# Attention decay on two engines: a split by diagonal block and rest in place of a split by key tile, and no mask matmuls in the transposed score pass

## The reference

```
scores = einsum('bhqd,bhkd->bhqk', q, k) / sqrt(8)
logw   = -log1p(softplus(decay_raw)[h] * log1p(max(q - k, 0)))
att    = softmax(scores + causal + logw[h])      # causal: -inf where k > q
y      = einsum('bhqk,bhkd->bhqd', att, v) @ w_proj
```

## Time and profile before

| | us |
|---|---|
| median of 3 runs | 771.75 (770.9 to 772.74) |
| span of the profiled execution, first to last instruction | 769.8 |
| TensorE busy | 648.5 (84%) |
| VectorE busy | 494.0 (64%) |
| GpSimd busy | 435.7 (57%) |
| ScalarE busy | 312.7 (41%) |

### The profile page before, as it was taken

The page is one execution under the profiler, slowest core; times in us unless marked ns, Lnnn a source line. Parts: engine busy times, 40 slices in busy tenths (PEclk is TensorE's granted clock), DMA queues, the critical chain, the costliest instruction groups (busy, mean ns, idle before and its releaser), DMA issues.

```text
span 769.8 us, 14013 instructions
## 1 busy us (share of the span) xinstructions
PE 648.5 (84%) x4380; PEld 427.1 (55%) x4381; DVE 494.0 (64%) x1115; ACT 312.7 (41%) x399; POOL 435.7 (57%) x295
## 2 busy tenths in 40 slices
PE   0392716999999899999899999998799999999950
PEld 0191415565665556666566656664376766767630
DVE  8618504887778677877678777786344544545535
ACT  3560003556555455555456555556222222222210
POOL 5210773686777667777577877787133333434332
PEclk9999856999999999999999999999699999999985
DMA  9920210021111111110111111013511111111119
GB/s 202 168 100 14 66 52 21 19 51 29 36 39 39 28 42 33 28 50 26 32 45 28 49 27 37 26 26 124 144 39 49 52 48 50 47 46 54 53 61 280
DMA packets 48299, 45.40 MB, mean 59 GB/s; under 512 B 6878, under 2 KB 38368, under 8 KB 47984
## 3 DMA queue, kind: packets, MB, share of 16 engines
q1 hardware_dynamic: 43888, 36.14, 19.4%
q0 software_dynamic: 4352, 8.47, 3.4%
HBM read 17.13 MB, written 17.44 MB: 45 GB/s over the span
## 4 chain that ended last, share of the span: by engine, by line
PE 80%; DVE 10%; another core or an unknown queue 3%; issue 2%; DMA 2%; POOL 1%; SPq 0%; ACT 0%; DVEq 0%; POOLq 0%
PE ps L1072 13%; PE psO L1145 11%; PE ps L1237 10%; PE ps L1115 10%; PE ps L1218 8%; PE ps L1227 4%; PE ps L1075 4%; PE psM L1027 4%; PE psM L1057 3%; PE ps L1118 2%; PE psM L1058 2%; PE psM L1043 2%; DVE neg_max L934 2%; PE psO L1034 2%
## 5 line engine op out<-in xcount | busy, mean ns | idle before, releaser
L464 POOL TENSOR_TENSOR probs<-probs,wdist 128x1024 f32<-128x1024 f32 (+1 forms) x124 | 275.5, 2226 | 110.8 <-ACT probs L709 110.5
L934 DVE TENSOR_REDUCE neg_max<-ps 128x1 f32<-128x512 f32 (+3 forms) x448 | 214.7, 531 | 99.5 <-PE ps L1075 79.1
L709 ACT ACTIVATE probs<-ps 128x1024 f32<-128x1024 f32 x160 | 163.9, 1025 | 155.0 <-PE ps L1118 118.1
L1072 PE MATMUL ps<-k_heads,q_rows 128*128 128x512 f32 (+3 forms) x512 | 141.5, 369 | 39.5 <-DVE neg_max L934 33.8
L650 POOL DMA_INDIRECT picked_dram<-values,k_heads x72 | 70.7, 982 | 129.9 <-DVE values L1001 126.9
L1072 PEld LDWEIGHTS ps<-k_heads,q_rows 128*128 128x128 f32 x512 | 88.5, 199 | 86.2 <-issue 49.0
L1115 PE MATMUL ps<-q_rows,k_heads 128*128 128x384 f32 (+3 forms) x512 | 119.4, 345 | 0.0
L745 ACT ACTIVATE probs<-ps 128x512 f32<-128x512 f32 x72 | 43.0, 597 | 144.9 <-PE ps L1218 144.9
L1145 PE MATMUL psO<-probs,values 128*32 128x512 f32 (+3 forms) x1024 | 97.3, 453 | 3.6 <-DVE probs L462 3.5
L1237 PEld LDWEIGHTS ps<-wdist,probs 128*128 128x128 f32 x576 | 70.6, 193 | 31.6 <-issue 31.2
L1075 PE MATMUL ps<-mask_q,ident_bf 128*128 128x256 bf16 (+1 forms) x320 | 86.2, 269 | 0.0
(11 more groups left out here) (157 smaller groups left out, 701.1 us busy)
## 6 DMA issues: line engine op xcount, KB each, us to landing
k_heads<-k_rows SPq DMA_DIRECT2D x128, 64.0 KB
rows_dram<-probs SPq DMA_DIRECT2D x1, 4680.0 KB, 36.2
k_heads<-rows_dram SPq DMA_DIRECT2D x72, 65.0 KB, 1.8
probs<-picked_dram SPq DMA_DIRECT2D x8, 512.0 KB, 7.4
send_rows<-xn_all SPq DMA_DIRECT2D x32, 65.5 KB, 1.9
wdist<-w1t SPq DMA_DIRECT2D x2, 1024.0 KB
out<-x_all SPq DMA_DIRECT2D x8, 256.0 KB, 5.1
xt_dram<-probs SPq DMA_DIRECT2D x6, 256.0 KB, 2.1
```

What stands on the lines that cost most here:

```text
L464: return eng.tensor_tensor(part, part, weights, ALU.mult)
L709: nc.scalar.activation(probs[:, at.ring(2), w, :], ps2[:, (at.c * P2_UNITS + w) % 2].rearrange("p a b -> p (a b)"), ACT.Exp).then_inc(exp_ ...
L934: last = nc.vector.tensor_reduce(dst, src, AX.X, ALU.max, negate=True)
L1072: mm(dst[:, 0:n], q[:, tile * P:n], k[:, quad, 0:n], start=first, stop=False)
```

## The change

The split of the decay is no longer by key tile. VectorE now takes in every unit the blocks of 128 queries on the diagonal (the first 128 columns of a tile's part), where values above the diagonal have to be cut by min(probs, 1) and the zeros of wdist: one instruction of 256 columns in units 0 and 1, two in units 2 and 3 (tile 1's first block, and tile 3, which is only a diagonal block), one of 512 in unit 4. GpSimd takes the rest of every unit: 768 columns in units 0 and 1, 512 in units 2, 3 and 4. So both engines now touch each unit, and each PV chunk waits for both.

With min(probs, 1) on every diagonal block, the 8 mask matmuls per group and mask_k are left out.

VectorE's steps move: units 0 and 1 of group n-2 come in slot n itself, after the reductions of P1 units 4 and 5; units 2 and 3, then unit 4, come one slot later, where tiles 3 and 2 stood. The special split of the last two groups goes away. The weight loads wait for all five units of both engines.

```diff
-TILE_UNITS = {0: (0, 1), 1: (2, 3), 2: (4,), 3: (2, 3)}
-TILE_COLS = {0: slice(0, 512), 1: slice(0, 384), 2: slice(0, 256), 3: slice(384, 512)}
+TILE_UNITS = {0: 2, 1: 4, 2: 5, 3: 4}
...
-    step("DW", n - 3, NGROUP, (1, 3))
+    step("DW", n - 3, NGROUP, (2, 3))
     step("P2", n - 2, NGROUP, 0)
...
-    step("DW", n - 3, NGROUP, (2,))
+    step("DW", n - 3, NGROUP, (4,))
...
     step("PV", n - 3, NGROUP, 2)
+    step("DW", n - 2, NGROUP, (0, 1))
...
+        def unit_cols(at, w, col, n):
+
+            k = 1024 // len(unit_heads(w))
+            return probs[:, at.ring(2), w, :].rearrange("p (h k) -> p h k", k=k)[:, :, col:col + n]
+
+        def unit_weights(at, w, dist, n):
 
             heads = unit_heads(w)
+            return wdist[:, at.g * QUADS + heads[0]:at.g * QUADS + heads[-1] + 1, dist:dist + n]
...
-                    sp.wait_ge(pool_probs, decay_done(last, 0 if 1 in dve_tiles(last) else 1)[1])
-                    sp.wait_ge(dve_probs, decay_done(last, 2)[1])
+                    sp.wait_ge(pool_probs, last.groups(P2_UNITS, P2_UNITS))
+                    sp.wait_ge(dve_probs, last.groups(P2_UNITS, P2_UNITS))
...
                     pool.wait_ge(exp_ready, at.groups(P2_UNITS, w + 1))
-                    apply_decay(nc.gpsimd, at, w, tile).then_inc(pool_probs, 1)
+                    n = (384, 384, 256, 256, P)[w]
+                    part = unit_cols(at, w, P, n)
+                    nc.gpsimd.tensor_tensor(part, part, unit_weights(at, w, P, n), ALU.mult).then_inc(pool_probs, 1)
...
+                    for w in units:
+                        dve.wait_ge(exp_ready, at.groups(P2_UNITS, w + 1))
+                        for col in ((0, 384) if w in (2, 3) else (0,)):
+                            part = unit_cols(at, w, col, P)
+                            last = nc.vector.scalar_tensor_tensor(out=part, in0=part, scalar=1.0,
+                                                                  in1=unit_weights(at, w, 0, P), op0=ALU.min,
+                                                                  op1=ALU.mult)
+                        last.then_inc(dve_probs, 1)
...
-                    for dst in masks:
-                        last = mask(dst)
                     last.then_inc(p2_full, 1)
...
-                    on_dve, done = decay_done(at, tile)
-                    pe.wait_ge(dve_probs if on_dve else pool_probs, done)
+                    pe.wait_ge(pool_probs, at.groups(P2_UNITS, TILE_UNITS[tile]))
+                    pe.wait_ge(dve_probs, at.groups(P2_UNITS, TILE_UNITS[tile]))
```

More of the change, by code:

```diff
@@ L96 @@
 LAST_SLOT = NGROUP + 5
[L99 to L109, removed]
 def slot_steps(n):
@@ L273, in build @@
         ident_bf = sb("ident_bf", [P, P], BF16)
-        mask_k = sb("mask_k", [P, P], BF16)
         mask_q = sb("mask_q", [P, 2 * P], BF16)
@@ L453, in unit_heads @@
             return range(QUADS) if w == 4 else range(2 * (w % 2), 2 * (w % 2) + 2)
-        def apply_decay(eng, at, w, tile):
+        def unit_cols(at, w, col, n):
+            k = 1024 // len(unit_heads(w))
+            return probs[:, at.ring(2), w, :].rearrange("p (h k) -> p h k", k=k)[:, :, col:col + n]
+        def unit_weights(at, w, dist, n):
             heads = unit_heads(w)
[L458 to L464, removed]
+            return wdist[:, at.g * QUADS + heads[0]:at.g * QUADS + heads[-1] + 1, dist:dist + n]
         def add_picked(engine, eng, batches, summed):
@@ L569, in _ @@
                 nc.gpsimd.memset(mask_q[:], 0.0).then_inc(pool_consts, 1)
-                nc.gpsimd.memset(mask_k[:], 0.0).then_inc(pool_consts, 1)
                 nc.gpsimd.memset(minus_half[:], -0.5).then_inc(pool_consts, 1)
@@ L576, in _ @@
                                ).then_inc(slot_table, 1)
-                pool.wait_ge(pool_consts, 5)
+                pool.wait_ge(pool_consts, 4)
                 nc.gpsimd.affine_select(out=ident[:], in_=ident[:], compare_op=ALU.is_equal, fill=0.0, base=0,
@@ L583, in _ @@
                                         pattern=[[0, 2], [-1, P]], channel_multiplier=1).then_inc(ident_ready, 1)
-                nc.gpsimd.affine_select(out=mask_k[:], in_=mask_k[:], compare_op=ALU.is_ge, fill=NEG, base=0,
-                                        pattern=[[1, P]], channel_multiplier=-1).then_inc(ident_ready, 1)
                 nc.gpsimd.iota(dist[:], pattern=[[1, SEQ]], base=0, channel_multiplier=-1,
@@ L629, in p2_step @@
                 def p2_step(at, w):
-                    tile = {0: 0, 1: 0, 2: 1, 3: 1}.get(w)
-                    if tile is None or tile in dve_tiles(at):
-                        return
                     if not at.looped and at.c < GROUPS:
@@ L758, in _ @@
                 nc.vector.tensor_tensor(dec_abs[:], decay_in[:], dec_neg[:], ALU.max).then_inc(dve_init, 1)
-                dve.wait_ge(ident_ready, 6)
+                dve.wait_ge(ident_ready, 5)
                 nc.vector.tensor_scalar(dist[:], dist[:], 0.0, None, ALU.max).then_inc(dve_init, 1)
@@ L840, in _ @@
                 dve.wait_ge(logits_ready, 1)
-                dve.wait_ge(ident_ready, 7)
+                dve.wait_ge(ident_ready, 6)
                 def first_of_best(src, top, pick):
@@ L955, in mt_step, with dw_step @@
                     nc.vector.tensor_tensor(q, psM[:], q.bitcast(F32), ALU.add).then_inc(misc_free, 1)
-                def dw_step(at, tiles):
+                def dw_step(at, units):
                     if not at.looped and at.c < GROUPS:
                         dve.wait_ge(wdist_causal, at.c + 1)
[L960 to L965, removed]
+                    for w in units:
[6 more added lines that the diff above has]
+                        last.then_inc(dve_probs, 1)
                 def nt_step(at):
@@ L1015, in _ @@
             def _(pe):
-                pe.wait_ge(ident_ready, 7)
+                pe.wait_ge(ident_ready, 6)
                 pe.wait_ge(w_rows_ready, 7)
@@ L1114, in scores @@
                         a = tile * P
[L1115 to L1120, removed]
+                        return mm(dst, k[:, quad, a:a + P], q[:, a:], start=first, stop=w not in (2, 3) or not first)
                     for s, quad in enumerate(unit_heads(w)):
                         if w < 2:
-                            scores(pair[:, s, :], 0, quad)
-                            masks.append(pair[:, s, 0:P])
+                            last = scores(pair[:, s, :], 0, quad)
                         elif w < 4:
                             scores(pair[:, s, 0:384], 1, quad)
-                            scores(pair[:, s, 384:512], 3, quad, first=False)
-                            masks.append(pair[:, s, 0:P])
+                            last = scores(pair[:, s, 384:512], 3, quad, first=False)
                         else:
                             last = scores(pair[:, s // 2, s % 2 * 256:s % 2 * 256 + 256], 2, quad)
-                    for dst in masks:
-                        last = mask(dst)
                     last.then_inc(p2_full, 1)
```

1 line of the change is left out of this document (removed).

## The result

The changed kernel takes 845.05 us (median of 4 runs, 844.12 to 845.57) beside 771.33 for the kernel before: ratio 1.0952 [1.0927, 1.0978], 73.7 us more. The forecast of 765.4 and its range of 756 to 779 are both wrong.

A forecast was written before the change was run, and what follows sets the result against it. It took TensorE's loop of slots to bound the kernel. Terms -7.8 (28 slots), +1.0, +0.9 and -0.5 summed to -6.4, a span of 763.4; with 1.95 from span to median, 765.4 us, range 756 to 779.

The forecast's parts named there:

- the bare slot's walk: Loop slot without V, KA, QA, YT or PJ work, timed instruction by instruction: 0.45 us longer, not 0.52 shorter.
- the others run free: Bare slot's start: after one 0.38 us wait, VectorE's remaining multiplies for units 2 and 3 run during GpSimd's send, done at 3.85.
- when both have work they alternate: VectorE and GpSimd elementwise work: each waits for the other's whole instruction, then they take turns.
- V and KA slots: Loop slots with 1.9 us more TensorE work than bare ones: no wait, 13.94 - 0.52 = 13.42 us.
- Rival 3: Loop: a GpSimd product falls among VectorE's four multiplies, P·V chunk 1 waits 1.27 to 1.82 us; slower, 777; 27%.
- the send sits in just that place: Argument against the slower case: GpSimd's row send, not a product, stands beside VectorE's four multiplies at the slot's start.
- The masks at 16.7: TensorE's loop: 256 mask matmuls at 0.065 us, at most 16.7 us to come back if nothing else waits.
- The batch of 51.2: Four loop slots together: 13.42 + 12.39 + 12.95 + 12.45 = 51.2 us, 1.1 less than 52.3.
- wait at unit 8: Bare slot: TensorE's P1 unit 8, due at 9.75, waits for VectorE's reductions until 10.3 to 10.5 us.
- Rival 1: The exclusion costs nothing on TensorE's path: the whole 16.7 us comes back, 755; 13%.
- the terms make -5.9: Loop stretch: 28 slots -7.8 us, slot 2 +1.0 and slot 31 +0.9.
- The tail, where I had -0.5: Slots 32 to 34: last P·V chunk can start at 543.1 against 543.71; -0.5 us, range -2 to +1.5.

The follow-up runs named there:

- e8: Separate kernel without the reference's computation: VectorE multiplies issued at varied delays against a GpSimd send or product and three products; multiply 0.41 or up to 4.66 us.
- e11: Separate kernel like that with three products, now four, with nothing, no-op, memset, or memset and wait between; multiply 5.34 with no-op, 0.42 with wait.
- e5: Changed kernel with GpSimd's unit 0 product waiting until VectorE's four multiplies of units 2 and 3 are done; 772.02 us, ratio 1.0014.
- e9: Changed kernel with a one-column memset and a wait for it behind each slot's GpSimd row send; 772.41 us, ratio 1.0015.
- e3: Changed kernel with GpSimd's row send moved from the slot's end to behind the product of unit 3; 796.86 us, ratio 1.0336.
- e1: Kernel before the change with only the mask matmuls left out, old split kept; 753.91 us, ratio 0.978.
- e6: Changed kernel with VectorE's seven multiplies per group replaced by reductions of the same columns to a spare column; 757.12 us, ratio 0.9813.
- e10: Changed kernel with both the memset and wait behind the send and GpSimd's unit 0 waiting for VectorE's four multiplies; 769.84 us, ratio 0.9981.

## Why the prediction was wrong, step by step

**The step that failed** is in the bare slot's walk: "then GpSimd sends a row (1.01) and the others run free", together with what it rests on, "when both have work they alternate". With products released behind the send, a multiply runs free only if it is issued within the send's first 0.30 us; at 0.36 or later it gets no turn, but waits until GpSimd stands still (e8, e11): 4.52 us in the loop, where the walk has 0.41. With nothing released behind the send it does run free (0.41 at 0.38 and 0.72 us into it, e5 and e9). The Trainium skill, in "SBUF — State Buffer", section "SBUF: two separate sides", states a lock that whoever starts first holds for its whole instruction. Behind a leading product the runs agree (1.78 beside one product of 1.80); behind a send one instruction's length is not the bound (4.66, through three products).

**Why the rows of before could not refute it.** The earlier trace rows show product behind product, where alternation is true. In the old bare slot the send ends at 323.28, the two multiplies come at 324.02, and GpSimd stands still for 1.24 us behind its send (1.25 to 2.27 in the next slots I read), because unit 0's exponential isn't there yet. The change moves both: unit 4 now has a product on GpSimd ahead of the send, which puts the send 1.74 us behind the start of VectorE's reductions (320.07, slot 15) where it was 0.55 ahead of it, and four multiplies stand there. The third falls 0.38 us into the send, the fourth 0.72. Whether one sticks is decided by the exponential of unit 0, which releases the product behind the send. In the loop, ready between 0.36 us before and 0.28 after the send's start, the third stuck; three times, ready at 0.28 or 0.29, the third got through and the fourth stuck; ready at 0.8, in the V and KA slots, none did. One stuck multiply delays P·V and the reductions, TensorE stands, and the clock falls.

**Rival 3 was the nearest** and had 27%: P·V chunk 1 does wait for VectorE in the loop. Its mechanism, one product between the four multiplies, is real, but it showed by itself only in e3 and in slots 3 and 4; e3 took 796.86, beyond the 784 of its worst case. Its "against it: the send sits in just that place" was the fault turned round: the send was the cause. I priced the send as a rest for the other engine, and had no row of a multiply waiting in one. There I should have put a bound, of waiting for all that GpSimd had released.

**What the runs split**, as ratios to before: 1.0952 less 1.0015 (e9) is 72 us for stuck multiplies and what follows from them. 1.0015 less 0.978 (e1) is 18 us for the new split without stuck multiplies. In the profiled executions 13.0 of it lie in the loop (395.2 against 382.3), and since e6's loop takes no longer than e1's, these are the ordinary turns and not VectorE's load. 2.2 are in the tail and 2.5 in the expert phase. Against the 18 stand the masks' 16.5.

**What was right.** The masks at 16.7 (e1: 16.5). Durations of 1.27, 1.82 and 0.41 (medians 1.28, 1.83 and 0.42). The batch of 51.2, which needs both that turns of one instruction are taken and that the cluster is left alone: 51.2 in e5 and in e9. Three of its slots are within 0.07, the bare one within 0.19, and its wait at unit 8 came where it was walked. Rival 1 is out with it: only with the multiplies gone (e6) is the bare slot 11.48.

**What was mis-sized, with the failed step put right.** e9 and e5 end at about 772, not at 765.4. The loop stretch, where the terms make -5.9, is 8.0 shorter in e5, but only 2.9 in e9: there slots 2 to 4, taken at about nothing in all, cost 3.05 (14.7, 13.84 and 13.84 against 14.05, 13.09 and 12.19). In e5 they take 14.03, 12.49 and 12.53. Slots 3 and 4 have no send ahead of the cluster, so e9 has no pause there: unit 0's product at 139.30 falls among the four multiplies, which take 3.16, and this is rival 3's mechanism, which e5's wait takes out. The walk was made for slots with a send and not redone for these two. The tail, where I had -0.5, costs 1.8 in e9 and, with its two stuck multiplies, 5.3 in e5. The expert phase, taken at nothing, is 1.0 (e5) to 1.9 us (e9) longer without a change in its code; over all kernels here, with that code the same, it takes 220.9 (e1) to 225.9 us (e6), and the longest ones (e6, e10) also have the most time at the granted clock of 0.50 (over 41 us, against 34 in e1).

**What stays open.** Why a multiply takes its turn between two products but not behind a send with a product released is not shown, only that it is so. Only this one indirect send was tried, so which property of it matters is open, and how long behind a send a multiply can still get stuck is known only up to 1.06 us into the first product. What lengthens the expert phase, and what slot 2 waits for in e9, was not tried. A version with the old split and no masks that is safe for scores of any size was not run.

## What to carry to other kernels

When two engines exclude one another, ask for each instruction that may wait not only how long the other's one instruction is, but how long the other goes on without standing still, and take that as the upper bound until a row shows that turns are taken. Behind a GpSimd send with released work after it, a short VectorE instruction with two SBUF inputs can cost the whole queue: keep it out of that place, or give GpSimd a real wait behind the send. And before moving work off the engine that bounds, try the removal alone: here leaving the masks out of the old kernel gave 16.5 us, and the new split built for it took away more than it gave.

## What the runs showed of the hardware

- A VectorE multiply of 256 columns with two SBUF inputs, issued 0.36 us or more into GpSimd's indirect send while products behind the send were already released, ended 0.28 us after the last of the products that followed without a gap: 4.66 us through three, 5.88 through four, 7.59 in the changed kernel's tail. So did two issued in the first product behind a send (5.29 and 6.80, e5).
- With no product released behind the send, one issued 0.36 to 0.38 us into it took 0.41 and was done 0.2 before the send's end; one issued 0.72 into it took 0.41 too (e5, e9, e11).
- A no-op (5.34) or a memset without a wait (5.38) behind the send changes nothing; with a memset and a wait for it the multiply is not stuck (0.42), and 0.08 us of idle GpSimd between two products freed one that was (3.45).
- The same multiply behind a leading product ended 0.3 us after that one, 1.78 in all. The next product then takes 1.44 instead of 1.26.
- Reductions of the same columns with one SBUF input in the multiplies' places made 757.12 us of 845.05.
